# Moving the first normalisation's statistics from VectorE to ScalarE, and the numerator's matmuls a quarter later

## What is computed

```python
x = x + xattn(layernorm(x), ctx, ctx)
    # q: softmax over the channels of a head; k: softmax over the sequence
    # kvs = einsum(k, v); out = einsum(q, kvs)
x = x + ffn(layernorm(x), router_w, A, B)
    # logits = x @ router_w.T; keep the 2 largest of 4; gates = softmax
    # delta = sum_e gates_e * 4 * (x @ A_e.T) @ B_e.T, rank 16
```

## Time and profile before

| what | value |
|---|---|
| median of 3 executions | 493.07 us (491.03 to 505.27) |
| profiled execution, its own time | 493.56 us |
| its span, first to last instruction | 491.8 us |
| busy in the span: PE, DVE, ACT, POOL | 404.7, 416.6, 241.4, 358.9 us |
| mean granted clock of TensorE | 0.944 |
| moved by DMA | 137.95 MB, 281 GB/s |

### The profile page before, as it was taken

One profiled execution on the slowest core, in us unless ns is written; L12 is line 12 of the kernel. 1 busy time (PEld: TensorE's weight loads), 2 busy tenths in 40 slices (PEclk: granted clock), 3 DMA queues, 4 the chain that ended last, 5 costly groups with the idle time before them and its releaser, 6 DMA issues.

```text
span 491.8 us, 22601 instructions
## 1 busy us (share of the span) xinstructions
PE 404.7 (82%) x9960; PEld 346.6 (70%) x9960; DVE 416.6 (85%) x1109; ACT 241.4 (49%) x340; POOL 358.9 (73%) x341
## 2 busy tenths in 40 slices
PE   5477877979988898879888898979889887989764
PEld 5466766868777677768776777868677676878543
DVE  2598888989998999899987999989999998976652
ACT  1155556545555455555555356545655556564100
POOL 1369997878888787878877787887878786985200
PEclk9568999999999998999998999999999999999955
DMA  8987686587979797787977698887879795532243
GB/s 332 427 329 291 253 315 259 205 311 285 345 263 344 273 390 255 263 332 297 379 279 296 260 331 336 286 316 274 320 282 367 267 384 213 195 152 91 112 188 128
DMA packets 24689, 137.95 MB, mean 281 GB/s; under 512 B 2192, under 2 KB 4368, under 8 KB 12176
## 3 DMA queue, kind: packets, MB, share of 16 engines
q1 hardware_dynamic: 24592, 136.51, 73.5%
HBM read 102.95 MB, written 33.55 MB: 278 GB/s over the span
## 4 chain that ended last, share of the span: by engine, by line
PE 39%; DVE 35%; issue 16%; DMA 4%; POOL 3%; ACT 2%; SPq 1%; DVEq 0%; POOLq 0%
DVE y_sb L631 9%; PE num_ps L367 8%; DVE max_n L566 8%; PE kv_ps L348 7%; PE kv_ps L398 6%; PE delta_ps L431 6%; PE raw_ps L384 6%; DVE bn_parts L582 4%; DMA sq_a<-in_bt_dram 4%; PE delta_ps L432 3%; DVE rden L619 3%; DVE attnT L622 3%; POOL y_sb L287 2%; DVE rz L611 1%; DVE midT L722 1%
## 5 line engine op out<-in xcount | busy, mean ns | idle before, releaser
L287 POOL TENSOR_TENSOR y_sb<-attnT,y_sb 128x512 f32<-128x512 f32 x128 | 164.6, 1286 | 78.6 <-DVE attnT L622 77.3
L275 POOL TENSOR_TENSOR ek_sb<-ctx_sb,kmax_row 128x512 f32<-128x512 f32 x128 | 167.5, 1311 | 15.7 <-ACT kmax_row L464 15.7
L431 PE MATMUL delta_ps<-midT,b_hi 128*128 128x256 f32 x256 | 83.3, 346 | 38.2 <-DVE y_sb L631 37.0
L367 PE MATMUL num_ps<-kv_sb,x_sb 64*64 64x65 f32 x4096 | 94.5, 228 | 8.6 <-issue 7.5
L631 DVE TENSOR_TENSOR y_sb<-delta_ps,y_sb 128x512 f32<-128x512 f32 x128 | 87.5, 683 | 15.8 <-PE delta_ps L432 15.3
L348 PE MATMUL kv_ps<-ctx_sb,ek_sb 128*64 128x65 f32 x2048 | 94.0, 234 | 7.0 <-issue 4.2
L566 DVE TENSOR_REDUCE max_n<-ctx_sb 128x32 f32<-128x512 f32 x128 | 86.4, 677 | 10.8 <-DMA ctx_sb<-in_ctxt_dram 10.4
L622 DVE TENSOR_TENSOR attnT<-num_ps,rden 128x512 f32<-128x512 f32 x128 | 88.5, 691 | 4.6 <-DVE rden L619 0.2
L348 PEld LDWEIGHTS kv_ps<-ctx_sb,ek_sb 128*64 128x64 f32 x2048 | 75.1, 140 | 22.9 <-issue 8.8
L367 PEld LDWEIGHTS num_ps<-kv_sb,x_sb 64*64 64x64 f32 x4096 | 75.2, 137 | 22.6 <-issue 15.0
L384 PE MATMUL raw_ps<-w_sb,y_sb 128*64 128x69 f32 x2048 | 86.6, 225 | 4.4 <-issue 4.4
(11 more groups left out here) (55 smaller groups left out, 324.7 us busy)
## 6 DMA issues: line engine op xcount, KB each, us to landing
ctx_sb<-in_ctxt_dram SPq DMA_DIRECT2D x32, 1040.0 KB, 5.6
x_sb<-in_x_dram SPq DMA_DIRECT2D x32, 1024.0 KB, 8.0
y_sb<-in_xt_dram SPq DMA_DIRECT2D x32, 1024.0 KB, 9.7
out_dram<-y_sb SPq DMA_DIRECT2D x30, 1024.0 KB, 5.9
out_dram<-y_sb SPq DMA_DIRECT2D x8, 256.0 KB, 2.1
sq_a<-in_bt_dram SPq DMA_DIRECT2D x1, 1024.0 KB, 18.5
w_sb<-in_wt_dram SPq DMA_DIRECT2D x1, 552.0 KB, 10.8
cst<-in_consts_dram SPq DMA_DIRECT2D x1, 145.0 KB, 2.3
```

The source lines that it names most:

```text
L275: pool.tensor_tensor(ek_sb[:, t % 2, chunks(g), :].rearrange("p (a b) c -> p a b c", b=2), ctx_sb[:, t % 4, 2 * g:2 * g + 2, 1:P + 1, :].r ...
L287: pool.tensor_tensor(y, attnT[:, g, :], y, ALU.add).then_inc(x1_made, 1)
L367: mm = pe.matmul(num_ps[n, h, j * (DH + 1):(j + 1) * (DH + 1)], x_sb[d, t % 4, c * P + half * DH:c * P + (half + 1) * DH], kv_sb[d, t % 2, ...
L431: pe.matmul(to, b_hi[:, j * P:(j + 1) * P], midT[:, p % 2, :], start=True, stop=False)
```

## The change

- The statistics of x leave VectorE. ScalarE makes a copy of the whole tile of x (to a place that nobody reads) with an accumulated sum (`sum_x`, in step 4t - 4), VectorE turns the sum into minus the mean (`ln1_mean`, step 4t - 3), ScalarE squares x minus the mean with an accumulated sum (`square_x`, step 4t - 2), and VectorE makes the variance of it (`ln1_var`, step 4t - 1). The copy's output grows from 128 to 2048 columns of bf16.
- `numerator`, `normalise` and `add_x` move from offset 4 to 5, `project` from 6 to 7, `kv_recip` from 3 to 4. In TensorE's step the numerator stands ahead of `kv`.
- In VectorE's step `mid_low` moves from the front to just ahead of `add_delta`, `kv_recip` to behind `max_part`; `add_delta` and `normalise` are behind `max_whole`, and the small steps of the first normalisation are last.
- GpSimd has `root1` first. ScalarE's squares of both halves are of tile T - 2, in its steps 0 and 1; the second half of the queries moves from step 0 to step 1.
- `load_x` moves from offset -8 to -7.

```diff
-                t, g = tile_at(q, -8)
+                t, g = tile_at(q, -7)
                 if t is not None and t >= 3 and g == 0:
                     after(sp, num_done, 4 * (t - 4) + 4)
                     load_x(t)
...
             for q in range(FIRST, LAST + 1):
+                root1(q)
                 shift(*tile_at(q, -3))
                 root2(q)
-                add_x(*tile_at(q, 4))
-                root1(q)
+                add_x(*tile_at(q, 5))
...
+                numerator(*tile_at(q, 5))
                 kv(*tile_at(q, 0))
-                project(*tile_at(q, 6))
+                project(*tile_at(q, 7))
                 fold_squares(q)
-                numerator(*tile_at(q, 4))
                 turn_mid(q)
...
+            def sum_x(t):
+                if not 0 <= t < NT:
+                    return
+                act.wait_ge(x_landed[t % 4], 16 * (t // 4 + 1))
+                after(act, x_squared, t)
+                act.activation(junk[:], x_sb[:, t % 4, :], ACT.Copy,
+                               accum_out=x_sum[:, t % 4:t % 4 + 1]).then_inc(x_summed, 1)
+
+            def square_x(t):
+                if not 0 <= t < NT:
+                    return
+                act.wait_ge(negmean1_made, t + 1)
+                act.activation(junk[:], x_sb[:, t % 4, :], ACT.Square, bias=negmean1[:, t % 4:t % 4 + 1],
+                               accum_out=x_sq[:, t % 4:t % 4 + 1]).then_inc(x_squared, 1)
...
                 if r == 0:
                     mid_high(q)
+                    square_x1(T - 2, 0)
                     copy_kv(T - 1)
-                    square_x1(T - 2, 1)
-                    queries(T - 1, 1)
+                    sum_x(T + 1)
                 if r == 1:
                     spread_row(T + 1)
                     keys(T, 1)
+                    square_x1(T - 2, 1)
+                    queries(T - 1, 1)
                 if r == 2:
                     gate_exp(q)
-                    square_x1(T - 1, 0)
+                    square_x(T + 1)
                 if r == 3:
                     copy_squares(T - 2)
                     keys(T + 1, 0)
...
-                dve.bn_stats(bn_parts[:, t % 4, g, :], x_sb[:, t % 4, cols(g)]).then_inc(bn_parts_made, 1)
...
+            def ln1_mean(q):
+                t, g = tile_at(q, -3)
+                if t is None or g:
+                    return
+                dve.wait_ge(x_summed, t + 1)
+                dve.tensor_scalar(negmean1[:, t % 4:t % 4 + 1], x_sum[:, t % 4:t % 4 + 1], -1.0 / N, None,
+                                  ALU.mult).then_inc(negmean1_made, 1)
+
+            def ln1_var(q):
+                t, g = tile_at(q, -1)
+                if t is None or g:
+                    return
+                dve.wait_ge(x_squared, t + 1)
+                dve.tensor_scalar(var1e[:, t % 4:t % 4 + 1], x_sq[:, t % 4:t % 4 + 1], 1.0 / N, EPS, ALU.mult,
+                                  ALU.add).then_inc(var1e_made, 1)
...
                 a, b, c = pair_at(q, 13), pair_at(q, 14), pair_at(q, 15)
-                mid_low(q)
                 if b is not None:
                     gate_beats(b, 0)
                 if c is not None:
                     gate_mid(c)
                 max_part(*tile_at(q, -8))
+                kv_recip(q)
                 if a is not None:
                     gate_centre(a)
                 if b is not None:
                     gate_beats(b, 1)
                     gate_mask(b)
-                ln1(q)
+                if not early:
+                    max_whole(q)
+                mid_low(q)
                 add_delta(*delta_at(q))
-                bn_part(*tile_at(q, -4))
                 if a is not None:
                     gate_logits(a)
                 if b is not None:
                     gate_rank(b)
-                if not early:
-                    max_whole(q)
-                kv_recip(q)
-                normalise(*tile_at(q, 4))
+                normalise(*tile_at(q, 5))
                 if a is not None:
                     gate_below(a)
                 if b is not None:
                     gate_select(b)
                     gate_sum(b)
                     gate_scale(b)
+                ln1_mean(q)
+                ln1_var(q)
                 ln1_bias(q)
```

More of the change, by code:

```diff
@@ L74, in xattn_lora_moe_kernel @@
         sq_sum = sb("sq_sum", [P, 2, P])
-        junk = sb("junk", [P, P], BF16)
+        junk = sb("junk", [P, N], BF16)
         max_n = sb("max_n", [P, 2, P])
@@ L81, in xattn_lora_moe_kernel @@
         rz = sb("rz", [P, 2])
-        bn_parts = sb("bn_parts", [P, 4, G, 6])
-        bn_out = sb("bn_out", [P, 4, 2])
+        x_sum = sb("x_sum", [P, 4])
+        negmean1 = sb("negmean1", [P, 4])
+        x_sq = sb("x_sq", [P, 4])
         var1e = sb("var1e", [P, 4])
@@ L142, in xattn_lora_moe_kernel @@
         row_made = sem("row_made")
+        x_summed = sem("x_summed")
+        x_squared = sem("x_squared")
         ek_made = sem("ek_made")
@@ L153, in xattn_lora_moe_kernel @@
         kmax_made = sem("kmax_made")
-        bn_parts_made = sem("bn_parts_made")
-        bn_made = sem("bn_made")
+        negmean1_made = sem("negmean1_made")
         var1e_made = sem("var1e_made")
@@ L575, in max_whole @@
                 dve.tensor_reduce(kmax[:, t % 2:t % 2 + 1], turn_ps[:, 0:P], AX.X, ALU.max).then_inc(kmax_made, 1)
-            def bn_part(t, g):
-                if t is None:
+            def ln1_mean(q):
+                t, g = tile_at(q, -3)
+                if t is None or g:
                     return
-                if g == 0:
-                    dve.wait_ge(x_landed[t % 4], 16 * (t // 4 + 1))
-                dve.bn_stats(bn_parts[:, t % 4, g, :], x_sb[:, t % 4, cols(g)]).then_inc(bn_parts_made, 1)
-            def ln1(q):
-                t, g = tile_at(q, 0)
-                if t is not None and g == 0:
-                    i = t % 4
-                    dve.wait_ge(bn_parts_made, 4 * t + 4)
-                    dve.bn_aggr(bn_out[:, i, :], bn_parts[:, i, :, :].rearrange("p g s -> p (g s)")).then_inc(bn_made, 1)
-                    dve.wait_ge(bn_made, t + 1)
-                    dve.tensor_scalar(var1e[:, i:i + 1], bn_out[:, i, 1:2], EPS, None, ALU.add).then_inc(var1e_made, 1)
+                dve.wait_ge(x_summed, t + 1)
[8 more added lines that the diff above has]
+                                  ALU.add).then_inc(var1e_made, 1)
             def ln1_bias(q):
@@ L598, in ln1_bias @@
                 dve.wait_ge(rstd1_made, t + 1)
-                dve.tensor_scalar(nbias1[:, i:i + 1], bn_out[:, i, 0:1], rstd1[:, i:i + 1], -1.0, ALU.mult,
+                dve.tensor_scalar(nbias1[:, i:i + 1], negmean1[:, i:i + 1], rstd1[:, i:i + 1], None,
                                   ALU.mult).then_inc(nbias1_made, 1)
             def kv_recip(q):
-                t, g = tile_at(q, 3)
+                t, g = tile_at(q, 4)
                 if t is None or g:
```

## The result

The changed kernel took 504.12 us (median of 4, 498.24 to 511.06) against 492.65 us before (median of 4): a ratio of 1.019, 95% interval 1.012 to 1.026. It is slower by 1 to 3%, where 5% faster had been forecast. The profiled execution took 504.25 us, with a span of 502.5.

A forecast was written before the change was run, and what follows sets the result against it. VectorE was taken to bound the kernel at 13.71 us per tile, TensorE afterwards at 12.6. From 493.6 us, 29 less in the steady part and 2 more at the start gave 466 us, range 453 to 488.

The forecast's parts named there:

- What bounds the kernel now: Steady tiles: VectorE is the bound, busy 12.70 of 13.71 us per tile, and the other engines wait for it.
- DVE's statistics go: VectorE per tile: 2.99 us of statistics leave, 0.15 is added, 12.70 falls to 9.86 us.
- ACT's new passes: ScalarE per tile: two passes over 2048 elements add 4.3 us (3.8 to 5.5), 7.41 becomes 11.7 us.
- The numerator ahead of `kv`: TensorE's step: VectorE's wait for the numerator (16.2 us in the steady stretch) goes; nothing is added to TensorE.
- Waits on ACT's results, DMAs, GpSimd: ScalarE's results reach VectorE 1 to 2 us early, transfers cost nothing, GpSimd stays at 11.12 us per tile.
- Start, fill and drain: Outside the steady tiles: 2 us more at the start, no change in the four fill tiles or the drain.
- The sum: Steady tile: TensorE's 11.84 busy, 0.68 "issue" and 0.1 of waits make 12.6 us, 29 us less in all.
- the slower one: Rival at `spread_row`: the keys' chain stuck behind ScalarE's statistics, 14.3 us per tile, 511 us; chance 0.10.
- Rival 1: Steady tiles: ScalarE takes the bound, 13.0 to 13.5 us per tile, 484 us (480 to 490); chance 0.20.
- rival 4: Steady tiles: VectorE's removed time is replaced by waits at the same 13.7 us pace, 495 us; chance 0.10.
- Rival 3: TensorE's "issue" gaps shrink too, leaving its bare 11.9 to 12.1 us per tile, 451 us; chance 0.10.
- the four signs: ScalarE over 95% with TensorE awaiting keys/kv; VectorE stalled at `x_sum`/`x_sq`; ScalarE awaiting x; new passes well over 2.45 us.

The follow-up runs named there:

- e6: Kernel before with all stores but the last pair's left out, a quarter of the traffic gone: 490.49 us, ratio 0.997.
- e4: Kernel before with the reordering alone, the statistics left on VectorE: 517.49 us, ratio 1.038.
- e1: Changed kernel with only the load of x put back at its old offset -8: 513.98 us, ratio 1.041.
- e11: Changed kernel with the numerator in matmuls of 128 stationary columns instead of twice 64, 492 instead of 620 instructions per tile: 471.24 us, ratio 0.954.
- e2: Changed kernel with all stores but the last pair's left out, a quarter of the traffic gone: 465.99 us, ratio 0.942.
- e7: Changed kernel with ScalarE's two statistics passes over 128 columns instead of 2048, statistics then wrong: 508.36 us, ratio 1.037.
- e8: Kernel before, its order kept, with only the statistics moved to ScalarE: 513.20 us, ratio 1.045.
- e5: Changed kernel with the store one step later and the load of turned x held back, to spread the transfers: 509.14 us, ratio 1.037.
- e9: Changed kernel with loads of context, x and turned x as four DMAs each and stores as two, in short rows: 501.29 us, ratio 1.015.
- e14: Changed kernel with the numerator wide for even chunks and in two halves for odd ones, 556 instructions per tile: 507.26 us, ratio 1.024.
- e3: Changed kernel with numerator and project each in one matmul of 128 stationary columns instead of two of 64: 540.13 us, ratio 1.073.

## Why the prediction was wrong

- *What bounds the kernel now*: right. VectorE held it at 13.71 us. Taking a quarter of the traffic away changed nothing (e6).
- *DVE's statistics go*: 9.86 us foreseen, 10.24 measured. The durations of its instructions fell by 2.87 us per tile, as foreseen (2.84); fewer of them overlap than before.
- *ACT's new passes*: 4.3 us foreseen. The rows of after:

```profile
L480 ACT ACTIVATE junk<-x_sb,negmean 128x2048 bf16<-128x2048 f32 x25 | 49.9, 1995 | 0.0
L473 ACT ACTIVATE junk<-x_sb 128x2048 bf16<-128x2048 f32 x26 | 49.6, 1907 | 0.0
...
L473 ACT ACTIVATION_READ_ACCUMULATOR junk<-x_sb 128x1 f32 x26 | 5.1, 197 | 0.0
L480 ACT ACTIVATION_READ_ACCUMULATOR junk<-x_sb,negmean 128x1 f32 x25 | 4.8, 193 | 0.0
```

  1.91 + 2.00 + 0.20 + 0.19 = 4.30 us. The accumulated sum costs one more instruction of 0.2 us, within the bounds of 0 and 0.31. ScalarE's total was 10.97, not 11.7, since instructions overlap more: their durations rose by 4.25 us per tile, and the overlapped part of them from 0.60 to 1.29.
- *The numerator ahead of `kv`*: half right. VectorE's wait for it fell only from 16.2 to 12.2 us. "Nothing is added to PE" held for its work; but the new order as a whole (e4) brought most of the added pauses, 22.5 of 34.9 us, and that cost was put at nothing.
- *Waits on ACT's results, DMAs, GpSimd*: no cost taken, none found in the waits. That the load of x matters in either place isn't shown (e1).
- *Start, fill and drain*: 2 us more were foreseen, none and none; they are 0.1, 2.1 and 1.0 us less.
- *The sum*: here it failed, at the term "PE: 11.84 busy plus the 0.68 of 'issue' that no slack absorbs any longer". I took the pauses for a fixed amount that a full TensorE merely exposes. They measured 2.09 us per tile. They are no fixed amount: they depend on TensorE's pace and on how soon the next packet comes. A block of 256 instructions lasted 5.50 us before and 5.08 after, and the next packet began to move 2.37 and 2.83 us after its start, so both moved towards the pause. The busy time rose too, from 11.84 to 12.07, with more stretches at the 1.2 GHz level after long pauses. That e11 and e2 take 12.80 us per tile, near the 12.6 forecast, and 471 and 466 us, is luck: e11 holds 1.7 us more matmul work per tile than the forecast's kernel, and e2 half of the pauses. The sum's 11.84 was too much for a TensorE that nothing stops (some 11.1 us, e11), as its 0.68 was too little.
- *The rivals*: the slower one had the sign and a chance of 0.10, and a wrong place. `spread_row` waits (12.2 us for TensorE's transpose), and e7 shows that ScalarE's load has no part in it. Its mechanism exists in e8, where the order is the old one. Rival 1 didn't happen (ScalarE is busy 77%), nor rival 4: the pace changed, and VectorE has slack. Rival 3 said that the pauses would shrink; that they could grow was in none, although their rows were in front of me: 17 of them, up to 2.3 us. I used their sum and never asked what they were. None of the four signs that I named for being wrong appeared either.
- *Range and chances*: 453 to 488 missed 504, and 0.70 on faster was too sure with the four engines foreseen within 1.7 us of each other and one term unexplained.

What stays open: why a packet takes as long as it does. Less traffic shortens it (e2, e6); breaking up the groups of three transfers or cutting their rows doesn't (e5, e9). Which of the requests waits for what inside a DMA engine, no view of the trace tells. Nor is it explained why the packets come later in the new order (2.70 us in e4, 2.83 after) than in the old one (2.37 before, 2.35 in e8), with the same bytes. The changed kernel wasn't run beside its variants, so differences of 1 or 2% between them aren't read.

## What to carry to other kernels

A pause of an engine that no semaphore explains is a cost with a cause: count instructions between such pauses and look whether packets of instructions land at their ends, before the pause is put into a sum as a constant. On a TensorE with many small matmuls the number of instructions is a resource beside the array's time; once the engine in front of it is relieved, fewer and wider matmuls can win even when they cost more array time. When a bound is lifted, ask at what pace the next engine will then run, and what feeds it at that pace. And try the parts of a change apart: here each alone lost as well, the order by pauses (e4), the statistics by waits (e8).

## What the runs showed of the hardware

- TensorE's program arrives in 16 KB packets of 256 instructions, on the DMA engines that move the data. Its instructions began 1.1 us or more after the landing, in every block from 80 to 440 us of all 18 traces.
- The next packet began to move 1.9 to 3.0 us after a block's start, on average, in the ten runs of the table, later where the data filled the DMA engines. Pauses were almost nil where a block lasted 6.5 us and more (e11, e14), and 2.09 us per tile where it lasted 5.08 (after).
- Two matmuls of 64 stationary columns cost far less than one of 128 with the same moving columns: a step's `project` of 69 columns 0.49 against 1.04 us, the numerator 0.62 against 1.04 (e3, e11). Alternating the two forms chunk by chunk cost 1.29 us (e14).
- A ScalarE pass with an accumulated sum is the pass (1907 ns for 2048 columns) plus an instruction of 197 ns that reads the sum (after).
